# One-hot adjacency and dense products in place of gathered edge rows in a two-layer graph network

## The reference

```python
# layer 0, beside an attention-like mixer on the same xn
xn = layernorm(x)
gathered = (xn @ W_neighbor)[src] * edge_weight[:, None]
x = x + xn @ W_self + segment_sum(gathered, dst) + bias + mixer0(xn)
x = x + moe0(layernorm(x))          # top 1 of 8 experts
# layer 1
xn = layernorm(x)
h = xn * rsqrt(max(out_degree, 1))[:, None]
agg = segment_sum(h[src], dst) * rsqrt(max(in_degree, 1))[:, None]
x = x + elu(agg @ weight + bias) + mixer1(xn)
x = x + moe1(layernorm(x))          # top 2 of 8 experts
```

## Time and profile before

| | us |
|---|---|
| runs | 3667.5, 3673.8, 3678.27 |
| median | 3673.8 |
| the profiled execution | 3669.23 |
| its span | 3667.5 |
| TensorE products busy | 2688.2 |
| GpSimd busy | 2386.7 |
| VectorE busy | 1117.2 |
| ScalarE busy | 495.0 |
| mean granted TensorE clock | 0.754 |

### The profile page before, as it was taken

How to read it: one execution, slowest core, us unless ns; L and a number is a source line. 1 busy time by engine, 2 the same in 40 slices (tenths; PEclk the granted TensorE clock), 3 DMA queues, 4 the chain that set the end, 5 groups by cost and what they waited for, 6 DMA issues and landing times.

```text
span 3667.5 us, 36489 instructions
## 1 busy us (share of the span) xinstructions
PE 2688.2 (73%) x9839; PEld 1991.9 (54%) x9840; DVE 1117.2 (30%) x3641; ACT 495.0 (13%) x1086; POOL 2386.7 (65%) x1966
## 2 busy tenths in 40 slices
PE   0689797787788787589837776868677786672887
PEld 0355576565566575478715544546445464451776
DVE  4444332233133222200042322332432434312111
ACT  0111010010010010123221000111010110010322
POOL 0678887887878877212128788878777788762454
PEclk9898776676676676689956877768757686675999
DMA  3544533433433433422135344433433334334343
GB/s 106 136 125 128 150 104 77 105 96 81 110 85 90 111 82 83 103 79 71 47 132 151 95 116 118 110 87 93 112 83 107 93 94 112 81 81 105 79 90 64
DMA packets 355030, 364.46 MB, mean 99 GB/s; under 512 B 203757, under 2 KB 282536, under 8 KB 354907
## 3 DMA queue, kind: packets, MB, share of 16 engines
q0 software_dynamic: 271104, 270.76, 29.9%
q1 hardware_dynamic: 77302, 86.00, 7.5%
q10 hardware_dynamic: 6500, 6.41, 0.6%
HBM read 291.95 MB, written 71.29 MB: 99 GB/s over the span
## 4 chain that ended last, share of the span: by engine, by line
POOL 41%; PE 25%; issue 14%; another core or an unknown queue 6%; DMA 5%; DVE 4%; SPq 2%; POOLq 1%; ACT 1%; DVEq 1%; ACTq 0%
POOL xg L546 38%; PE bank L647 23%; DMA xg<-feat,idx_cur 3%; PE bank L653 2%; POOL sorted_in L599 2%; POOL xg L552 1%; DVE oh L1355 1%; DMA feat<-arena 1%; SPq L376 1%; DMA xg<-feat,idx_tail 1%; POOLq L537 0%; POOLq L532 0%; SPq L449 0%; SPq L447 0%
## 5 line engine op out<-in xcount | busy, mean ns | idle before, releaser
L546 POOL DMA_INDIRECT xg<-feat,idx_cur x1600 | 1976.4, 1235 | 559.4 <-issue 433.0
L647 PE MATMUL bank<-xg,oh 125*125 125x256 f32 (+1 forms) x3324 | 1083.9, 482 | 510.5 <-DMA xg<-feat,idx_cur 410.7
L647 PEld LDWEIGHTS bank<-xg,oh 125*125 125x125 f32 x3324 | 737.5, 234 | 832.3 <-DMA xg<-feat,idx_cur 583.1
L653 PE MATMUL bank<-ident,arena 125*128 125x125 f32 x700 | 170.8, 374 | 305.5 <-remote 202.7
L647 PE MATMUL bank<-t,w_h 128*128 128x250 f32 (+1 forms) x1184 | 330.4, 433 | 14.8 <-remote 8.0
L1358 DVE TENSOR_SCALAR oh<-iota,dst_cur 125x125 f32<-125x125 f32 x800 | 190.4, 355 | 412.2 <-PE bank L647 409.0
L653 PEld LDWEIGHTS bank<-ident,arena 125*128 125x128 f32 x700 | 103.4, 187 | 371.2 <-issue 367.9
L647 PEld LDWEIGHTS bank<-t,w_h 128*128 128x128 f32 x1184 | 232.8, 202 | 110.1 <-issue 58.5
L1355 DVE TENSOR_SCALAR oh<-iota,dst_cur,w_cur 125x125 f32<-125x125 f32 x800 | 232.3, 428 | 133.7 <-PE bank L647 129.6
L647 PE MATMUL bank<-arena 125*125 125x25 bf16 (+2 forms) x1000 | 236.1, 397 | 17.5 <-DVE arena L1495 17.5
L647 PEld LDWEIGHTS bank<-arena 125*125 125x125 bf16 (+1 forms) x1000 | 225.5, 311 | 31.0 <-issue 25.6
(11 more groups left out here) (258 smaller groups left out, 2241.3 us busy)
## 6 DMA issues: line engine op xcount, KB each, us to landing
xg<-feat,idx_cur POOLq DMA_INDIRECT x1600
sorted_in<-pad_rows POOLq DMA_DIRECT2D x16, 878.4 KB, 17.2
arena<-sorted_in SPq DMA_DIRECT2D x49, 251.0 KB
arena<-rows_b SPq DMA_DIRECT2D x5, 1875.0 KB
w_exp<-in_L_ffn_Wd POOLq DMA_DIRECT2D x8, 1024.0 KB
w_exp<-in_L_ffn_W POOLq DMA_DIRECT2D x16, 512.0 KB
arena<-in_x SPq DMA_DIRECT2D x10, 625.0 KB
feat<-arena SPq DMA_DIRECT2D x10, 625.0 KB
```

The lines of the kernel that those rows point to most:

```text
L546: pool.indirect_dma_start(xg[:, s, 0:D], None, feat, bass.IndirectOffsetOnAxis(ap=idx_cur[g % 2][:, s:s + 1], axis=0)).then_inc(xg_full[s ...
L647: return pe.matmul(o, w, r, start=first, stop=last, skip_group_check=not check)
L653: return pe.transpose(ps[:, at:at + n], src, ident[0:n, 0:n])
```

## The change

The gathers of edge rows are gone, but for one tail in each block. Features of all nodes are kept in SBUF (`xg[:, 0:25, :]`, node = 125 c + partition). For a block of 125 target nodes the kernel makes the 3125 x 125 adjacency on chip, in 25 pieces of 125 x 125, and multiplies each by its piece of the features.

To make it, each node has 64 slots for its run of edges. Once, in the attention loop, GpSimd fetches the tile in which each node's run begins and then a window of 64 edges for each node (50 indirect DMAs in all; a windowed copy of the edge list comes as an additional input). VectorE turns a window into five bf16 rows (src // 125 + 1 or 0 where the edge is another node's; src modulo 125; the weight as a sum of three bf16 numbers), TensorE transposes them (`turn_slots`), ScalarE copies and stores them to DRAM (`keep_slots`), and later GpSimd's queue loads 82 KB of them for each block (`slots_in`). Partitions 0 to 63 hold the slots of one node of a pair, partitions 64 to 127 those of the other.

For a block, VectorE makes in four groups of 16 pairs bf16 one-hots `row_hots` [128, 125, 16] and `col_hots` [128, 50, 16] and in layer 0 also three weighted copies of the latter. TensorE then has for each of 64 pairs one product (layer 1), or one for the out-degree count and three for the weight (layer 0). Eight pairs fill the bank `ps_kv` with 400 columns; ScalarE copies them to `adj`, f32, two buffers. The adjacency of block b + 1 is made in the same `aggregate` that multiplies the one of block b: eight pairs, then three dense products, eight times.

```diff
+            def adjacency(layer, k, half):
+                if half == 0:
+                    take(pe, hot_full[k])
+                take(pe, adj_ps_free)
+                for i in range(GJ):
+                    j = GJ * half + i
+                    if layer == 0:
+                        mm(ps_agg[0:B, 260:260 + HW], row_hots[k][:, :, j], col_hots[k][:, :, j], False, False, False)
+                    for n in range((3, 1)[layer]):
+                        col = col_hots[k] if layer else wcol_hots[k][:, n, :, :]
+                        last = mm(ps_kv[0:B, HW * i:HW * i + HW], row_hots[k][:, :, j], col[:, :, j],
+                                  n == 0, n == (2, 0)[layer])
+                last.then_inc(adj_ps_full, 1)
+                if half == 1:
+                    zero(ps_agg, 16, False, False).then_inc(hot_free[k], 1)
...
             def aggregate(b, par, layer, before, groups=ALL, first=False, last=False):
...
                 for k in groups:
-                    take(pe, oh_full[k])
-                    for s in range(GS * k, GS * k + GS):
-                        if s % GL == 0:
-                            pe.wait_ge(xg_full[s // GL], landed)
-                        last = mm(ps_agg[0:B, 0:cols], oh[:, s, :], xg[:, s, 0:cols], s == 0, False, False)
+                    for half in range(2):
+                        g = 2 * k + half
+                        if not last:
+                            adjacency(layer, k, half)
+                        for c in range(3 * g, NB if g == 2 * GR - 1 else 3 * g + 3):
+                            mm(ps_agg[0:B, 0:cols], adj[par][:, c, 0:B], xg[:, c, 0:cols], False, False, False)
...
+            def turn_slots(groups):
+                for g in groups:
+                    take(pe, slot_made)
+                    for i in range(G):
+                        take(pe, agg_free)
+                        for n in range(5):
+                            o = ps_agg[:, SL * n:SL * n + SL]
+                            mm(o, slot_src[:, i, n, SL:3 * SL], ident_b[0:B, 0:SL], True, False)
+                            last = mm(o, slot_src[:, i, n, 0:2 * SL], ident_b[0:B, SL:2 * SL], False, True)
+                        last.then_inc(agg_full, 1)
...
+            def keep_adjacency(par, groups=ALL):
+                for k in groups:
+                    for half in range(2):
+                        g = 2 * k + half
+                        take(act, adj_ps_full)
+                        o = adj[par].rearrange("p c (h j) -> p j h c", h=2)[:, GJ * g:GJ * g + GJ, :, :]
+                        act.activation(o, ps_kv[0:B, 0:HW * GJ].rearrange("p (j h c) -> p j h c", j=GJ, h=2),
+                                       ACT.Copy).then_inc(adj_ps_free, 1)
...
             def onehots(b, layer, groups=ALL):
...
+                    for h in range(2):
+                        tt(row_hots[k][:, :, GJ * h:GJ * h + GJ], row_no,
+                           cur[:, 1, j0 + GJ * h:j0 + GJ * h + GJ].unsqueeze(1).to_broadcast([128, B, GJ]), ALU.is_equal)
+                    last = tt(col_hots[k], col_nos,
+                              cur[:, 0, j0:j0 + 2 * GJ].unsqueeze(1).to_broadcast([128, HW, 2 * GJ]), ALU.is_equal)
+                    if layer == 0:
+                        chain(last)
+                        for n in range(3):
+                            last = tt(wcol_hots[k][:, n, :, :], col_hots[k],
+                                      cur[:, 2 + n, j0:j0 + 2 * GJ].unsqueeze(1).to_broadcast([128, HW, 2 * GJ]), ALU.mult)
```

More of the change, by code:

```diff
@@ new lines, in gather @@
+            def gather(layer, b, feat, before):
+                if b + 2 < NB:
+                    slots_in(layer, b + 2)
+                lo = pool.value_load(lo_tab[0:1, b:b + 1], min_val=0, max_val=NT - 1)
+                n = pool.value_load(tail_n[0:1, b:b + 1], min_val=1, max_val=MAXT)
+                begin = pool.value_load(cum_tab[0:1, b:b + 1], min_val=0, max_val=MAXT * NB)
+                with pool.Fori(0, n) as c:
+                    at = nc.s_assert_within(pool.snap(lo + c), 0, NT - 1,
+                                            skip_runtime_bounds_check_because="a block's last tile lies inside the list")
+                    take(pool, tail_free)
+                    pool.dma_start(edge_tail[:, :], a["edges"][ds(at * B, B), :]).then_inc(tail_in, 16)
+                    pool.wait_ge(tail_in, pool.snap((before + begin + c + 1) * 16))
+                    pool.sem_inc(tail_known, 1)
@@ L709, in aggregate, with open_sums, first_adjacency @@
+            def open_sums():
+                take(pe, agg_free)
+                zero(ps_agg, 260 + HW, True, False)
+            def first_adjacency(layer):
+                open_sums()
+                for k in ALL:
+                    for half in range(2):
+                        adjacency(layer, k, half)
+            def aggregate(b, par, layer, before, groups=ALL, first=False, last=False):
+                cols = D + layer
                 if groups[0] == 0:
-                    take(pe, agg_free)
+                    if not first:
+                        open_sums()
+                    if last:
+                        take(pe, adj_ps_free)
@@ L804, in experts @@
                     pe.sem_inc(bank_free, 1)
-            take(pe, tabs_ready)
             zero(ps_kv, 512, True, False)
-            zero(ps_agg, D + 1, True, True)
-            with pe.Fori(0, NS) as s:
+            for s in range(NS):
                 take(pe, v_full)
@@ L1604, in layer0 @@
                 dve.sem_inc(v_full, 1)
+                tail(1)
+                hots(1)
+                tail(2)
                 hots(2)
-                degs(2)
-                hots(3)
                 take(dve, ps_full)
@@ L1766, in mixer, with graph @@
                 dve.sem_inc(rowb_used, 1)
-                beside("sums", b, plan)
+                beside("sums", s, plan)
                 chain.restart()
-            def graph(s, b, plan):
-                for j, groups in plan.get("aggs", ()):
-                    tails(b + j, False)
+            def graph(s, plan):
                 take(dve, aggs_in, 16)
@@ L1833, with edge_rows @@
 L1_ffn_W1 L1_ffn_b1 L1_ffn_W2 L1_ffn_b2""".split()
+def edge_rows(dst, src, weight):
+    import numpy as np
+    edges = np.stack([np.ascontiguousarray(v).view(np.int32) for v in (dst, src, weight)], axis=1)
+    after = np.tile(np.array([[-1, 0, 0]], np.int32), (SL, 1))
+    at = np.arange(0, E + 1, WS)[:, None] + np.arange(SL)[None, :]
+    windows = np.concatenate([edges, after])[at]
+    return edges, windows.transpose(0, 2, 1).reshape(len(at), 3 * SL).copy()
 def kernel(**inputs):
```

650 lines of the change are left out of this document (384 added, 266 removed).

## The result

The changed kernel takes 4945.9 us (median of 3 runs, 4945.5 to 4952.3) where the kernel before takes 3673.8 us: 1.347 times as long, with a 95% interval of 1.345 to 1.349. The forecast was 5000 us, within 4050 to 5350. The profiled execution has a span of 4944.3 us. Parts 1 and 4 of its page answer to the earlier trace rows: busy us (share of the span) xinstructions, then the chain of waits by engine and by line.

The account below looks back on a forecast made before the run. The gather was taken to set the pace of the graph sums, with TensorE 77% full meanwhile. Terms of 4134 us replace 2799 us, +1335 on 3669 us: 5004, said as 5000 us, range 4050 to 5350.

Parts of the forecast that it names:

- Small products: TensorE, both layers: 8000 products making the adjacency, each paced by its own weight load of 0.225 us, 1800 us.
- Dense products: TensorE, adjacency times features: layer 0 at the low clock, 0.427 us a record, 534 us; layer 1 at 0.35, 437 us.
- No sharing of loads: TensorE's small products: one weight load counted for each, also where four products have equal weights.
- ScalarE: Copies of adjacency banks, 0.5 or 0.85 us each: hidden in layer 0, 20 us of stalls in layer 1, 36 before first blocks.
- VectorE: One-hots at 153 ns + 0.52 ns a column, 14.5 us a block in layer 0, 7.7 in layer 1, hidden: cost nothing.
- The bare steps and the slots: Attention steps without covering block passes 220 us, 48 us bare cost; slots for 25 blocks, about 4 us each, 100 us.
- The projection loop: Layer-1 projection loop without covering block passes: 165 us for five steps, 50 us more than TensorE's work and waits.
- A: Rival: small products at 0.107 us, as a contiguous load shows; 944 us less, 4060 us; chance 0.12.
- C: Rival: loads at 0.107 us and full clock in both layers, dense products 537 us; 3626 us; chance 0.04.
- B: Rival: moving columns add to the load, 0.262 us a small product, or a 32-byte step is dearer; 5300 us; chance 0.10.
- D: Rival: a node's run over 64 slots sends all edges through the one-tile tail, over 10 ms; chance 0.01.
- The turn to the faster side: Small products: at full clock the change turns from slower to faster at a pair price of about 0.112 us.

Follow-up runs that it names:

- the first kernel of series: TensorE alone, graph network left out: 13 series of 96 small bf16 products, each changing step, width or moving columns; 0.074 us a product up to 4 bytes, 0.23 from 16.
- the run with 0.108 us: The changed kernel with the row one-hots laid out so that a product's 125 weight columns lie side by side; 3875.5 us, 1.056 of before.
- the series of 25, 50 and 100: TensorE alone, 96 small products each with 25, 50 or 100 moving columns and 125 weight columns 32 bytes apart; 0.232, 0.233 and 0.234 us a product.
- 0.070 (3468): The changed kernel with row and column one-hots both stored one column after another, still 125 row columns; 3467.9 us, 0.944 of before.
- the last kernel: The changed kernel with row one-hots 128 columns wide, and row and column one-hots both stored in pairs, columns 4 bytes apart; 3131.1 us, 0.851 of before.

## Why the prediction was right

**The mechanism.** TensorE replaced the gather as the bound, by the weight loads of the small products, as predicted. The sign and the size came out, 4946 against 5000 us. In the bare sum: 4279 us of TensorE work forecast (2688 - 1084 - 180 + 1800 + 534 + 437 + 64 + 20), 4243 measured; the rest 723 forecast, 701 measured. That this is so close is luck in part: the terms below miss by 50 to 100 us each, in both directions.

**Small products, 1800 us forecast.** The pace is 0.2325 us where I took 0.225 from the earlier trace rows; busy time 1896 us, which holds the ends that lie beside the dense products. The reason that I gave (data type, width and kind of step are the degree row's) was better than I knew. Two of the three carry the price, and I had a reason for one of them only: the step makes 0.233 us of 0.058 at full clock and of 0.107 at half (125 columns), and the missing three columns make 0.233 of 0.062 (32 bytes apart) and 0.058 of 0.025 (neighbours). The data type was not tested. I wrote that the load hides 50 moving columns because they cost at most what the weights do per column, 0.09 us. They cost 0.093 to 0.095, so that step was a little short, without effect on the result. That the pace is the same at both clock levels holds: 0.233 at both. The 40- and the 32-byte step are nearly alike: 21.1 and 22.4 us for 96 in the first kernel of series.

**Dense products, 534 and 437 us.** Layer 0 measured 590: the clock was the low one, as the earlier trace rows said, and the records overlap the small ones beside them, so that some of the 56 us is counted twice. Layer 1 measured 387: the clock was mostly the high one (0.86 from 3600 to 4600), so 0.31 us a record where I took 0.35, nearer the low level than was right.

**No sharing of loads.** 16781 loads for 16780 products, and 0.244 us for each counting product left out.

**ScalarE.** A copy takes 859 ns, which is the upper of my two values; the group of the small products above shows 31.1 us of TensorE waiting for it, against 20 us in layer 1 and 18 before the first blocks (2 x 8 x 1.1) forecast. Its row:

```profile
L1112 ACT ACTIVATE w_adj<-bank 125x400 f32<-125x400 f32 x400 | 343.5, 859 | 2425.9 <-PE bank L689 2425.5
```

**VectorE.** 676 ns for 1000 columns and 571 for 800, where 0.153 + 0.52 ns a column says 673 and 569. Hidden, as forecast.

**The bare steps and the slots.** The attention loop ends at 372 after 246 us with 100 us of idling; I had 220 us for the steps. For the slots I had 100 us with nothing beside, 4 us a block. The turns of the last 20 blocks go from 397 to 441, 44 us, and within a group of five they follow each other every 1.47 us, so that term was twice too big; the 108 us from 372 to 480 also hold sums over the nodes before the slots and the first adjacency behind them. The projection loop is 145 us, 165 forecast.

**Order of the stages.** Layer 0 ends at 2933 instead of the 2880 that I named; layer 1 gained 63 us where I had it lose some tens. Of that difference its dense products give 50 us and the projection loop 20; the rest was not followed up. The two errors have opposite signs and the total hides them.

**The rivals.** A (0.107 us a product, 4060 us) and C (the same with the full clock, 3626) fell with the pace of 0.233 us. They came closer for a layout that this kernel has not got: the run with 0.108 us takes 3875, with a clock from 480 to 1000 of 0.61, between the two. B (5300) fell with the 4922 us of contiguous moving columns and with the series of 25, 50 and 100. D did not happen. The turn to the faster side that I set at 0.112 us under full clock did not come at 0.108 (3875; the clock was not full) and had come at 0.070 (3468).

What I had not seen is that the width matters as much as the step (1090 and 1070 us, each alone). The Trainium skill says it (TensorE: Matmul & The Clock Gate, section Weight-path perf modes): a fast weight load is on when the weights are 128 columns and not FP32, packed or strided. I weighed that page's section LDWEIGHTS against the row and passed this one over; the runs agree with it, 0.059 us for 127 neighbouring columns and 0.025 for 128, both at full clock, and with a 32-byte step 0.233 for 125 and 0.062 for 128.

So the price is in a missing padding of three columns and in a layout, and the change as such need not lose: in the last kernel the small products shrink from 1896 us to 289, and the dense ones of layer 0 go from 590 to 331 us as the granted clock in their stretch rises from 0.52 (580 to 1300) to 0.93 (480 to 1000).

## What to carry to other kernels

A product with few moving columns can cost its weight load, so read the weights' layout before the arithmetic. Make the loaded matrix full width (pad 125 to 128) and keep its columns, and the moving ones, within 4 bytes of each other; a layout in pairs served TensorE and VectorE alike here. Compare paces at the same clock level. A factor that a test shows to cost nothing may only be hidden under a larger one: test it again when that is gone.

## What the runs showed of the hardware

- With 128 neighbouring bf16 weight columns a product of 50 moving columns came every 0.025 us at full clock (0.041 at half), with 127 or 125 every 0.059 or 0.058 (0.107 at half), with 112 every 0.052 and with 96 every 0.045 (full clock). The full width was a case of its own at every step tried (32 bytes: 0.062 against 0.233 us).
- The step cost next to nothing to 4 bytes. At 8 bytes 96 products took 11.3 us, where they took 7.1 with neighbours, for 125 weight columns (3.4 and 2.6 us for 128), and 4.6 against 2.6 us for 50 moving columns. Over 16 bytes little was added (22.0 and 22.4; 5.9 and 6.1; moving 8.9 and 9.1 us).
- Loads of under 128 neighbouring columns followed the granted clock (0.058 and 0.107 us); loads and moving columns 16 or 32 bytes apart did not (0.232 and 0.233, 0.060 and 0.060, 0.093 and 0.093).
- With load and moving columns both at work, the longer set the pace: 0.093 us at full clock, where the two are 0.058 and 0.093, and 0.107 at half, where they are 0.107 and 0.093.
- VectorE's product with a broadcast operand in bf16 took 571 ns for 800 columns with inner runs of two or of sixteen and 987 ns where the innermost dimension read one value again and again.
- ScalarE's copy of 400 f32 columns out of PSUM with a permuted write took 859 ns, where the plain one of 500 columns took 590.
- The granted clock was 0.52 from 580 to 1300 with the slow loads, TensorE busy 99% of the time, and 0.93 from 480 to 1000 with the quick ones, TensorE busy 92% (476.69 of 520 us): it was not the engine's gaps that held it down.
